# A post-norm decoder of two layers: where TensorE makes the values in the two head loops

## What is computed

```python
# self-attention, causal, 512 keys
scores = jnp.einsum('bnqh,bnkh->bnqk', q, k) / scale
scores = jnp.where(causal, scores, jnp.finfo(scores.dtype).min)
attn = jax.nn.softmax(scores, axis=-1)
ctx = jnp.einsum('bnqk,bnkh->bnqh', attn, v)
# cross-attention, 1601 keys
scores = jnp.einsum('bhqd,bhkd->bhqk', qh, kh) * scale
attn = jax.nn.softmax(scores, axis=-1)
out = jnp.einsum('bhqk,bhkd->bhqd', attn, vh)
```

## Time and profile before

| | us |
|---|---|
| median of 3 runs | 1524.35 |
| lowest and highest | 1521.37, 1524.93 |
| the profiled execution's own time | 1521.03 |
| its span, first to last instruction | 1519.3 |

### The profile page before, as it was taken

One profiled execution on the slowest core, in us unless ns is written; L12 is line 12 of the kernel. 1 busy time (PEld: TensorE's weight loads), 2 busy tenths in 40 slices (PEclk: granted clock), 3 DMA queues, 4 the chain that ended last, 5 costly groups with the idle time before them and its releaser, 6 DMA issues. The chain is left out here.

```text
span 1519.3 us, 24902 instructions
## 1 busy us (share of the span) xinstructions
PE 1383.4 (91%) x9358; PEld 755.5 (50%) x9358; DVE 1065.5 (70%) x2320; ACT 775.2 (51%) x1067; POOL 337.8 (22%) x425
## 2 busy tenths in 40 slices
PE   6898899989999979848998889999999999999985
PEld 3565488847898966413434422333333333332374
DVE  4987466661212128667994799999999999996176
ACT  2344366621111102325674316788778878878654
POOL 3110322252000037643435420000000000000142
PEclk9999899999999989858999869999999999999999
DMA  9548533366898922764431650342223332220001
GB/s 343 181 144 246 155 131 124 121 215 217 273 302 272 306 83 56 215 200 121 132 87 39 187 167 5 88 102 69 66 66 77 96 90 66 66 66 1 1 1 56
DMA packets 153353, 198.69 MB, mean 131 GB/s; under 512 B 16235, under 2 KB 125311, under 8 KB 153106
## 3 DMA queue, kind: packets, MB, share of 16 engines
q1 hardware_dynamic: 141516, 165.34, 36.2%
q0 software_dynamic: 9200, 29.64, 6.4%
q10 hardware_dynamic: 2518, 2.13, 0.4%
HBM read 136.08 MB, written 60.70 MB: 130 GB/s over the span
## 5 line engine op out<-in xcount | busy, mean ns | idle before, releaser
L2122 DVE TENSOR_REDUCE xa_part<-psum 128x1 f32<-128x512 f32 (+1 forms) x768 | 471.2, 672 | 25.7 <-PE psum L1975 23.6
L2074 ACT ACTIVATE xa_P<-psum 128x1024 f32<-128x1024 f32 (+1 forms) x416 | 403.2, 1020 | 109.7 <-PE psum L1999 109.3
L1999 PE MATMUL psum<-sa_Q,xa_K 48*128 48x512 bf16 (+3 forms) x1664 | 264.9, 380 | 4.0 <-DMA sa_Q<-xa_mrow 3.0
L1975 PE MATMUL psum<-xa_K,sa_Q 48*128 48x512 bf16 (+1 forms) x768 | 241.5, 393 | 4.3 <-DVE xa_part L2122 2.0
L2015 PE MATMUL psum<-xa_P,xa_V 128*32 128x512 f32 (+1 forms) x1664 | 222.7, 607 | 0.4 <-ACT xa_P L2074 0.4
L1975 PEld LDWEIGHTS psum<-xa_K,sa_Q 48*128 48x128 bf16 x768 | 59.2, 94 | 240.7 <-DVE xa_part L2122 173.1
L1999 PEld LDWEIGHTS psum<-sa_Q,xa_K 48*128 48x128 bf16 (+3 forms) x1664 | 101.9, 97 | 77.5 <-ACT xa_P L2074 20.9
L2119 DVE CUSTOM_DVE_ANT_0 psum<-psum,cf_sb 128x512 f32<-128x512 f32 (+3 forms) x256 | 119.5, 521 | 26.3 <-PE psum L1975 25.6
L1328 PEld LDWEIGHTS psum<-xtT,wgu 128*128 128x128 f32 x992 | 115.5, 192 | 5.8 <-issue 4.6
L1328 PE MATMUL psum<-xtT,wgu 128*128 128x128 f32 x992 | 115.9, 275 | 1.4 <-issue 0.8
L2074 ACT ACTIVATE sa_P<-psum 128x1024 f32<-128x1024 f32 (+3 forms) x128 | 83.5, 702 | 44.8 <-PE psum L1999 44.6
(11 more groups left out here) (244 smaller groups left out, 2147.1 us busy)
## 6 DMA issues: line engine op xcount, KB each, us to landing
wgu<-in_f_gu SPq DMA_DIRECT2D x31, 1024.0 KB, 5.9
xa_K<-kx SPq DMA_DIRECT2D x192, 100.1 KB, 5.0
wdn<-in_f_dn SPq DMA_DIRECT2D x31, 512.0 KB, 6.2
vx<-xv_v SPq DMA_DIRECT2D x48, 256.0 KB, 3.4
xa_V<-vx POOLq DMA_DIRECT2D x16, 768.0 KB, 6.5
sa_Q<-qs SPq DMA_DIRECT2D x64, 96.0 KB, 2.3
sa_K<-ks SPq DMA_DIRECT2D x64, 96.0 KB, 2.3
sa_Q<-qx SPq DMA_DIRECT2D x64, 96.0 KB, 2.3
```

What stands on the lines that cost most here:

```text
L1975: last = pe.matmul(out[:, 0:width], hb.q(u)[tile:tile + HALF, to, qt * P:(qt + 1) * P], hb.k(u)[tile:tile + HALF, to, cut[e]:cut[e] + widt ...
L1999: last = pe.matmul(out(j), hb.k(u)[tile:tile + depth, to, kt * P:kt * P + r], hb.q(u)[tile:tile + depth, to, q0(kt):L], start=(half == 0), ...
L2074: act.activation(Pr[0:r, (u * KT + kt) % PR, h:h + 2, 0:w_], S_PS(p)[0:r, :, 0:w_], ACT.Exp, scale=SCALE).then_inc(s_exp, 1)
L2122: dve.tensor_reduce(part[:, g % 2, col + qt, e:e + 1], src[:, 0:cut[e + 1] - cut[e]], AX, ALU.max).then_inc(s_1free, 1)
```

## The change

In each key tile the order on PE is first pair of scores, values of the key tile before, second pair of scores, where it was first pair, second pair, values. It holds for both loops, since both use `group`. At key tile 0 the values are those of the last key tile of the group before, as they were. The units keep their places: one after the first turn, one after the second, two after the third.

```diff
                             point = kt * TURNS + turn
                             if turn == 0:
                                 scores(g, u, kt, 0, first)
-                            elif turn == 1:
+                            elif turn == 2:
                                 scores(g, u, kt, 2, first)
                             elif kt >= 1:
                                 values(g, u, kt - 1, first)
                             elif before:
                                 values(g - 1, (u + R - 1) % R, KT - 1, None)
```

## The result

The changed kernel takes 1711.82 us (median of 5 runs, 1695.14 to 1715.06) against 1524.33 us before (5 runs): a ratio of 1.1225 with a 95% interval of 1.1187 to 1.1263, 187 us slower. The profiled execution is the shortest of the five, 1695.14 us with a span of 1693.4; its mean granted clock is 0.932, that of the other four 0.909 to 0.916.

A forecast was written before the change was run, and what follows sets the result against it. No engine had much left, so the chain that closes one key tile was taken to decide. Cross loop +123 us and causal loop +47.5 us, 170 in all, gave 1692 us, with a range of 1650 to 1750.

The forecast's parts named there:

- The cycle: Cross loop, each key tile: values, unit, second pair, exponential and release follow one another, 2.99 us against 2.44.
- the start of ACT: Cross loop: delay from the modelled end of the second pair to ACT's exponential, 0.11 us of the 2.99.
- The terms once per group: Cross loop: three additions to each group, 0.50, 0.47 and 0.3 us, giving a group of 40.1 us.
- (a): Cross loop, key tile 0: values wait for ACT's copy of the output behind the second exponential, 0.50 us per group.
- (b): Cross loop, key tile 9: ACT's copy of the row of maxima delays a unit ahead of the values, 0.47 us.
- (c): Cross loop: the transposition of the maxima stands between unit and second pair in one tile, 0.3 us per group.
- The causal loop: POOL's triangle adds 0.75 us to each tile's chain; groups of 11.05 us against 8.16, +47.5 us in all.
- The clock: Rival: PE's waits in the causal loop lower the clock to 1.2 GHz; 1753 us, 1722 if in half; chance 0.13.
- own signs of being wrong: Values waiting for nothing, an interval below 36 us, or the granted clock leaving 1.00 in either loop.
- Shorter loop: Rival: second pair's exponentials come earlier, so the cycle over DVE decides; 1549 us, or 1594 with seven slots; chance 0.07.
- Faster: Rival: values fill PE's wait for ACT in the last cross and causal groups; 6 us less, 1518; chance 0.03.
- Six slots stayed six: Both loops: units stay at the same points, so six matmul slots remain between two values, at no cost.

The follow-up runs named there:

- e2: New order in the causal loop only, the cross loop keeping the order of the kernel before; 1601.77 us, ratio 1.0533 against the kernel before.

## Why the prediction was right, point by point

**The cycle.** Right, and nearly its size: 2.94 us a cross key tile in place of 2.99, with 1.00 for the values (1179.42 to 1180.42), 0.83 for unit and second pair, 1.02 for the exponential and 0.05 for the release. What was mis-sized is the start of ACT: 0.04 us after the modelled end of the pair (1183.37 + 0.82 = 1184.19; 1184.23) in place of 0.11. In rows 3 and 8 the last score was the only one on its tile, and its modelled end says less than its start; 0.05 x 208 is 10 us.

**The terms once per group.** The border's key tile is longer by 0.54 us (predicted 0.50), that of key tile 9 by 0.73 (0.47 + 0.3). Moving the copies took 0.45 and 0.47 of them away, so (a) and (b) are shown. What is left at key tile 9 is 0.26; that it is the transposition, the 0.3 of (c), is argued from what is left over, and no run moved the transposition. A group is 39.50 us (40.1), the last two together 72.0 (74.7), the first +1.3 (3). The cross loop got 112 us longer by itself, where 123 was predicted.

**The causal loop.** At full clock a group is 10.95 us (11.05). The triangle is in the cycle, as the run without it shows. The copy of the output was said to be hidden by it with 0.2 us to spare; without the triangle it is what the values wait for.

**The clock.** This is the step that was chosen wrongly between two cases. The forecast took the clock to stay at 1.00, and the fall stood as a rival with 0.13: the clock may fall in the causal loop, +30 us if in half of it. It did, in part: the causal loop alone costs 79 us where 47.5 was predicted, and 32 of them went with matmuls that keep PE busy; the 47 that are left are what was forecast. One of the prediction's own signs of being wrong, a granted clock that leaves 1.00 in either loop, thus came true. The reason given against it, that the last group of before waited for POOL at a clock of 1.00, was weak: that is one group behind a full stretch, not sixteen in a row, and in the changed kernel the same group runs at 0.50. So the forecast of 1692 us was 20 too low, as the sum of -11 in the cross loop and +31 in the causal one. That it came within 20 is in part luck: the cross loop's miss took off a third of the causal loop's.

**The rivals.** Shorter loop: out, the values do wait; the loop that it names appears once the cycle is open, at 2.49 us. Faster: right about where, and out as a whole. In the last two groups of the cross loop the place between the pairs does shorten things when the values are old enough (56.0 us with them two behind and the copies moved, against 57.2), and in the causal loop a group falls from 8.16 to 7.88.

**Row tiles.** Six slots stayed six: at 2.49 us a key tile there is no room for the seventh of 0.215 on top of 2.44. The Trainium skill's rule of strict order (TensorE: Matmul & The Clock Gate, section "The mechanism") is again not what the trace shows. The prediction's pair of starts (1143.20 and 1143.21) doesn't prove it by itself, for two starts in a row can be in program order. The single records do: behind the unit at 1180.42 the scores start at 1180.43, 1180.65, 1180.65 and 1180.87, and the one that signals ACT, the last of the four in the program, is the third of them; its modelled end is 1181.03, that of the fourth 1181.24.

## What to carry to other kernels

When a consumer is moved in the program of its engine, ask not how many signals it waits for but which of its own engine's earlier work has to come first: here the same count was asked for one place sooner, and a latency of two engines that lay beside the work came into the loop. Idle time on the other engines is then no slack; one small instruction ahead of a signal tells in one run whether it is. And an order that lets TensorE pause in every step can cost a second time, through its clock, as in the causal loop here; in the cross loop of the changed kernel, with shorter pauses, it did not.

## What the runs showed of the hardware

- The lower clock came and went within one loop with an even rhythm of work. In the causal loop of e2 it is 0.70 of full over 157 us; a group takes 10.95 us at the upper level and 13.62 at a mean of 0.63, 24% more, though more than half of the predicted cycle is spent in ACT and POOL.
- Matmuls whose results nobody reads made the program 32 us faster (1601.77 to 1570.08), with the clock at 1.00 (2.4 GHz) from 707 to 831 us, where it was 0.70 without them.
- The cross loop with pauses of 0.38 us in PE's matmuls in each 2.94 us kept its clock; with 1.35 us in 3.91 it fell in some groups and held at its upper level, 2.4 GHz, in others (intervals of 51.46 us).
- The two row tiles run ahead of each other. Of the four scores behind a unit in the program, the second, on the other tile, starts 0.01 us after the unit (1180.42 and 1180.43); the first, on the unit's tile, only at 1180.65. Which record is which follows from the signal that the last of the four carries (1180.65) and from the distance of some 0.22 us between starts on one tile.
